# Gate logits out of the attention's own products, all splits on GpSimd, and the first expert choice split in two parts

## The reference, cut to what matters

```python
x = x + tanh(g_xattn[0]) * xattn0(layernorm(x), ctx)       # one head, softmax over 120 keys
x = x + tanh(g_ffn[0]) * moe(layernorm(x))
x = x + tanh(g_xattn[1]) * xattn1(layernorm(x), ctx)       # 16 heads
x = x + tanh(g_ffn[1]) * fp8_linear(layernorm(x))

def moe(x):
    logits = x @ gate_w.T + expert_bias                    # 12 experts
    top, idx = top_k(logits, 2); w = softmax(top)
    # experts 0..7: y = silu(x @ w1.T) @ w2.T, experts 8..11: y = x
    return sum of w * y over the two chosen
```

## Time and profile before

| | |
|---|---|
| median of three executions | 374.39 us |
| the profiled execution, first to last instruction | 378.3 us |
| TensorE, VectorE, ScalarE, GpSimd busy | 92%, 69%, 58%, 41% |
| granted TensorE clock, mean | 0.964 |

### The profile page before, as it was taken

How to read it: one execution, slowest core, us unless ns; L and a number is a source line. 1 busy time by engine, 2 the same in 40 slices (tenths; PEclk the granted TensorE clock), 3 DMA queues, 4 the chain that set the end, 5 groups by cost and what they waited for, 6 DMA issues and landing times.

```text
span 378.3 us, 9027 instructions
## 1 busy us (share of the span) xinstructions
PE 348.3 (92%) x2959; PEld 279.9 (74%) x2960; DVE 261.1 (69%) x659; ACT 219.8 (58%) x452; POOL 154.3 (41%) x197
## 2 busy tenths in 40 slices
PE   3997889988999999999999998879999999998995
PEld 2776769756799999999999994556676667666674
DVE  2588984685646556654554447888789888957696
ACT  2589856742444544554454452456767787774586
POOL 6279967204355556555555535412130331101100
PEclk9999975598999999999999999999999999999999
DMA  6999902221133333322322213410110100000005
GB/s 180 327 413 419 419 30 83 86 84 49 50 99 111 125 108 102 123 83 71 81 69 76 76 40 114 154 57 2 57 58 11 50 2 2 2 5 0 2 28 196
DMA packets 15386, 38.25 MB, mean 101 GB/s; under 512 B 3574, under 2 KB 4748, under 8 KB 13820
## 3 DMA queue, kind: packets, MB, share of 16 engines
q1 hardware_dynamic: 10556, 26.74, 19.5%
q0 software_dynamic: 3936, 10.45, 9.4%
q10 hardware_dynamic: 864, 0.66, 0.6%
HBM read 24.34 MB, written 13.50 MB: 100 GB/s over the span
## 4 chain that ended last, share of the span: by engine, by line
PE 77%; DVE 12%; ACT 5%; DMA 3%; issue 2%; POOL 0%; POOLq 0%
PE two L1964 15%; PE two L1977 14%; PE two L2113 5%; PE two L1996 4%; PE two L2143 4%; PE two L2178 4%; PE two L2099 4%; PE two L2079 3%; PE two L1814 2%; PE two L1987 2%; PE two L2170 2%; PE two L1790 1%; DVE negmax L1133 1%; DMA ident<-in_c_ident 1%; PE two L2159 1%
## 5 line engine op out<-in xcount | busy, mean ns | idle before, releaser
L1364 DVE SCALAR_TENSOR_TENSOR gate<-th,two 128x512 f32<-128x512 f32 x39 | 26.8, 688 | 58.3 <-ACT th L842 32.5
L842 ACT ACTIVATE th<-two 128x512 f32<-128x512 f32 x39 | 23.4, 599 | 71.0 <-PE two L1977 52.8
L585 POOL DMA_INDIRECT y_d<-y_sb,goal_i x39 | 38.5, 988 | 50.4 <-ACT y_sb L852 50.4
L579 POOL DMA_INDIRECT xg<-xn_d,slot_i x39 | 38.0, 974 | 32.3 <-DVE slot_i L1315 14.8
L1964 PE MATMUL two<-wh,gh 128*128 x156 | 44.2, 283 | 0.1
L1964 PE MATMUL two<-wh,gl 128*128 x156 | 44.0, 282 | 0.0
L1964 PE MATMUL two<-wl,gh 128*128 x156 | 43.8, 281 | 0.0
L599 POOL TENSOR_TENSOR rstd<-var,half 128x2 f32<-128x2 f32 x14 | 9.9, 708 | 76.7 <-DVE var L1431 76.7
L1464 DVE TENSOR_REDUCE nm<-two 128x8 f32<-128x960 f32 x32 | 36.1, 1152 | 4.5 <-PE two L2099 4.1
L544 POOL TENSOR_TENSOR wl<-wl,wh 128x512 fp32r<-128x512 f32 x26 | 34.2, 1337 | 8.1 <-ACT wh L726 8.1
L1977 PE MATMUL two<-wh,xh 128*128 x78 | 34.2, 438 | 1.4 <-DVE xl L1358 1.4
(11 more groups left out here) (298 smaller groups left out, 883.3 us busy)
## 6 DMA issues: line engine op xcount, KB each, us to landing
wl<-in_wmoe SPq DMA_DIRECT2D x8, 1024.0 KB, 14.2
y_d<-wh SPq DMA_DIRECT2D x4, 1024.0 KB
yg<-y_d SPq DMA_DIRECT2D x7, 512.0 KB, 3.4
xn_d<-xq SPq DMA_DIRECT2D x8, 256.0 KB, 2.0
xz<-xn_d SPq DMA_DIRECT2D x8, 256.0 KB
out_x<-of SPq DMA_DIRECT2D x8, 256.0 KB, 2.0
x_sb<-in_x SPq DMA_DIRECT2D x1, 1024.0 KB, 10.1
x_sb<-in_x SPq DMA_DIRECT2D x1, 768.0 KB, 4.7
```

Of the source, the lines that this page charges most:

```text
L579: pool.indirect_dma_start(xg[:, n % 2, :], None, xn_d, bass.IndirectOffsetOnAxis(ap=slot_i[:, n:n + 1], axis=0)).then_inc(gathered[n % 2], 16)
L585: pool.indirect_dma_start(y_d, bass.IndirectOffsetOnAxis(ap=goal_i[:, n:n + 1], axis=0), y_sb[:, n % 2, :], None).then_inc(y_stored[n % 2] ...
L842: nc.scalar.activation(th[:], bank[2 + k][:], ACT.Tanh, scale=0.5).then_inc(th_ok, 1)
L1364: dve.scalar_tensor_tensor(gate[:, k, :], th[:], 1.0, bank[2 + k][:], ALU.add, ALU.mult).then_inc(gate_ok, 1)
```

## The change

- The keys of each batch get 12 more columns, which hold the centred gate weights (kq, pitch KP), and the values 12 more, which hold the values times the gate (vg, VP). So scores0 and attend give the gate's product with old x and with the attention's result; VectorE keeps the first (xgate), adds the second in add_x1, and logits_of multiplies the sum by the inverse root. The bias is added later, for seven batches at once and for the last by itself. transpose_x1, copy_xT1 and gate_of go.
- The bias and gain of the values go into their matmul (a second, two-row matmul), and ScalarE copies the values instead of VectorE.
- Each row of x has its inverse root and its negative mean times that root beside it (pitch XP = 258). Rows are stored unnormalised; norm_of normalises each gathered block on VectorE. norm1 goes. The reloads of xz go too: the loop scales x in place (keep_x, add_x).
- All 32 low parts are GpSimd's, in another order. Its inverse roots come one batch at a time, each behind two or one splits; ten splits stand behind the last root and ahead of the first gather, four more between the first gathers.
- VectorE makes the first choice for 14 tiles between the logits of batch 6 and those of batch 7, and for the last two tiles behind them. The maxima are scaled by two 1-wide products instead of one 2-wide with two tensors.
- TensorE waits for 25 low parts ahead of the expert loop's start, and for all 32 ahead of its first pair of second-layer products.

The diff, cut to its core:

```diff
+XP = D + 2
+KP = LK + 12
+VP = D + 12
...
-        ROOTS0, ROOTS1 = ((0, 1), (1, 4), (4, 8)), ((0, 2), (2, 4), (4, 6), (6, 7), (7, 8))
+        ROOTS0, ROOTS1 = ((0, 1), (1, 4), (4, 6), (6, 8)), tuple((b, b + 1) for b in range(B))
...
-        VECTOR_LOW = (6, 10, 14, 18, 22, 26)
+        FIRST_LAYER = [j for j in range(20, CHUNKS) if j % 4 < 2]
+        SECOND_LAYER = [j for j in range(20, CHUNKS) if j % 4 > 1]
+        HIGHS = list(range(20)) + FIRST_LAYER + SECOND_LAYER
+        LOWS = list(range(19)) + FIRST_LAYER + [19] + SECOND_LAYER
...
+            def low(n):
+
+                pool.wait_ge(split_h, HIGHS.index(LOWS[n]) + 1)
+                c = cols(LOWS[n], CHUNK)
                 pool.tensor_tensor(wl[:, c], wl[:, c].bitcast(F32), wh[:, c], ALU.subtract).then_inc(split_l, 1)
+
+            def lows(lo, hi):
+                for n in range(lo, hi):
+                    low(n)
...
+            root1(3)
+            lows(12, 14)
+            root1(4)
+            lows(14, 16)
+            root1(5)
+            low(16)
+            root1(6)
             low(17)
-            for j in range(19, 22):
-                low(j)
-            for j in range(23, 25):
-                low(j)
-            root1(1)
-            low(25)
-            low(27)
-            root1(2)
-            for j in range(28, 30):
-                low(j)
-            root1(3)
-            low(30)
-            root1(4)
-            low(31)
+            root1(7)
+            lows(18, 28)
...
+            gather(0)
+            gather(1)
+            lows(28, 30)
+            gather(2)
+            gather(3)
+            low(30)
+            gather(4)
+            low(31)
+            gather(5)
...
+            copy_probT(2)
+            spread_std(5)
+            high(8)
+            copy_v0(3)
+            copy_xT(5)
             high(9)
-            copy_probT(1)
-            for j in range(10, 12):
-                high(j)
-            exp0_of(2)
-            for j in range(12, 14):
-                high(j)
-            copy_probT(2)
-            high(14)
-            exp0_of(3)
+            exp0_of(4)
+            copy_probT(3)
...
+                dve.wait_ge(gsum_done, 1)
+                at = kq[:, :, 0:C * KP].rearrange("p b (c k) -> p b c k", k=KP)[:, :, :, LK:KP]
+                total = bank[4][:, 0:E_ALL].unsqueeze(1).to_broadcast([P, B, E_ALL])
+                for c in range(C):
+                    own_gate = gate_sb[:, c, 0:E_ALL].unsqueeze(1).to_broadcast([P, B, E_ALL])
+                    ins = dve.scalar_tensor_tensor(at[:, :, c, :], total, 2.0 / D, own_gate, ALU.mult, ALU.add)
+                ins.then_inc(gate_ok0, 1)
...
+                at = bank[6 + b % 2][:, 0:U * KP].rearrange("p (u k) -> p u k", u=U)
+                own.mark(dve.tensor_reduce(lowest[:, b % 2, :], at[:, :, 0:LK], AX, ALU.max, negate=True))
+                dve.tensor_copy(xgate[:, b], at[:, :, LK:KP])
                 own.settle()
-                dve.tensor_tensor(negmax[:, b % 2, :], lowest[:, b % 2, :], rstd0[:, b, :], ALU.mult).then_inc(max_done, 1)
+                for u in range(U):
+                    ins = dve.tensor_scalar(negmax[:, b % 2, u:u + 1], lowest[:, b % 2, u:u + 1], rstd0[:, b, u:u + 1], None,
+                                            ALU.mult)
+                ins.then_inc(max_done, 1)
...
+                own.mark(dve.reciprocal(rsum[:], at[:, :, VP]))
                 own.settle()
+                for u in range(U):
+                    dve.scalar_tensor_tensor(xgate[:, b, u, :], at[:, u, D:VP], rsum[:, u:u + 1], xgate[:, b, u, :], ALU.mult,
+                                             ALU.add)
...
+                    ins = dve.tensor_scalar(logit[:, cols(2 * b + u, E_ALL)], xgate[:, b, u, :], x_rstd(2 * b + u), None, ALU.mult)
                 ins.then_inc(logit_kept, 1)
+
+            def bias_logits(lo, hi):
+
+                dve.wait_ge(gate_in, 32)
+                dve.wait_ge(logit_kept, hi)
+                at = logit[:, lo * U * E_ALL:hi * U * E_ALL].rearrange("p (t e) -> p t e", e=E_ALL)
+                dve.tensor_tensor(at, at, gbias_sb[:, 0:E_ALL].unsqueeze(1).to_broadcast([P, U * (hi - lo), E_ALL]),
+                                  ALU.add).then_inc(biased, 1)
...
+            def choose_first(t):
+                highest(0, lg, t)
+                mark_highest(0, lg, t)
+                keep_first(0, t)
+                leave(t)
...
+            logits_of(5)
             add_x1(7)
-            logits_of(5)
             stats1(7)
-            low(22)
             logits_of(6)
-            low(26)
+            bias_logits(0, B - 1)
+            dve.wait_ge(biased, 1)
+            EARLY, LATE, ALL = slice(0, U * (B - 1)), slice(U * (B - 1), TILES), slice(0, TILES)
+            choose_first(EARLY)
             logits_of(7)
-
+            bias_logits(B - 1, B)
             dve.memset(pairs[:, TILES, :], 0.0)
-            dve.wait_ge(logit_kept, B)
-            highest(0, lg)
-            mark_highest(0, lg)
-            keep_first(0)
-            leave()
-            highest(1, left[:])
-            mark_highest(1, left[:])
-            keep_first(1)
+            dve.wait_ge(biased, 2)
+            choose_first(LATE)
+            highest(1, left[:], ALL)
+            mark_highest(1, left[:], ALL)
+            keep_first(1, ALL)
...
+            def norm_of(i, k):
+                wait(dve, gathered[k], 16 * (i + 1))
+                wait(dve, xgT_done, 2 * i + k - 1)
+                dve.tensor_scalar(xq[:, k, :], xg[:, k, 0:D], xg[:, k, D:D + 1], xg[:, k, D + 1:D + 2], ALU.mult,
+                                  ALU.add).then_inc(xq_ok, 1)
...
+                    t = 2 * i + (k - 4)
+                    dve.tensor_scalar(x_tile(t), x_tile(t), keep_x[:, cols(t, 1)], add_x[:, cols(t, 1)], ALU.mult, ALU.add)
...
+                dst = values_bank(b)[0:LK, 0:VP]
+                pe.matmul(dst, ctxT_sb[:, cols(b, LK)], vg[:], start=True, stop=False, skip_group_check=True)
+                pe.matmul(dst, pair1[:, 0:LK], bv2[:], start=False, stop=True, skip_group_check=True).then_inc(v0_done, 1)
...
+                    dst = bank[6 + b % 2][:, u * KP:(u + 1) * KP]
                     for c in range(C):
-                        ins = pe.matmul(dst, xT[:, b, c, u, :], kq[:, b, cols(c, LK)], start=False, stop=c == C - 1,
-                                        skip_group_check=True)
+                        pe.matmul(dst, xT[:, b, c, u, :], kq[:, b, cols(c, KP)], start=c == 0, stop=False,
+                                  skip_group_check=True)
+                    ins = pe.matmul(dst[:, 0:LK], spread0[:, b % 2, u, :], kq[:, b, C * KP:C * KP + LK], start=False,
+                                    stop=True, skip_group_check=True)
...
+            transpose_x0(4)
+            transpose_prob(2)
+            values0(3)
+            attend(2)
+            scores0(4)
+            transpose_x0(5)
+            transpose_prob(3)
+            values0(4)
+            attend(3)
+            scores0(5)
...
-            pe.wait_ge(split_l, CHUNKS - len(VECTOR_LOW))
-            pe.wait_ge(split_d, len(VECTOR_LOW))
+            pe.wait_ge(split_l, LOWS.index(FIRST_LAYER[-1]) + 1)
...
+            pe.wait_ge(split_l, CHUNKS)
```

613 lines of the change are left out of this document (278 added, 335 removed).

## The result

The changed kernel took 389.65 us (median of 4 executions, 388.36 to 392.78) against 374.41 for the kernel before on the same chip (4 executions, 371.9 to 377.45): a ratio of 1.043, 95% interval 1.034 to 1.052. It is slower. The forecast of 380.5 had the direction, the range of 369 to 386.5 did not hold the time. All ratios leave out executions that took over 1.5% more than the fastest of their kernel; the medians do not.

What follows compares the result with a forecast made beforehand. The prediction took the front ahead of the expert loop as deciding, TensorE having no idle time in the loop. Pairs 4.6 us later, clock 1.0 and ramp 0.5 made 384.4 of span 378.3, less 3.9 gave 380.5 us; range 369 to 386.5.

Steps and rivals of the forecast that it cites:

- the mechanism: Choice of experts: ten GpSimd splits take turns with VectorE's two-SBUF-input operations, so pairs stand at 82.6, 4.6 us later.
- the 12-wide products: Products making the logits on VectorE, one SBUF input: taken as not held by splits, 0.37 us for two.
- The alternative with two more turns: If the 12-wide logits products are held as well, the second choice runs after the last split; pairs at 83.6.
- the last batch: End of the attention: last batch's statistics, then logits(6) done at 67.1, where before the logits waited until 73.4.
- My chain of 5.5 us a batch: Attention, from one attend to the next: scores, transposes, copies, high part, exponentials, attend and handovers take 5.5 us.
- third rival: Attention: the clock falls early, adding 3.5 us from 52 on or 9 from 38 on; 384 to 390, chance 0.13.
- Behind the pairs: From pairs to the end: 1.0 us for TensorE's half clock plus 0.5 for splits and normalised rows among the gathers.
- the clock's 1.0: From pairs to slots: TensorE at half clock after a 12 us wait, 1.0 us taken between 0 and 4.
- The ramp: First gathers and transposes: two splits between gathers and normalised rows cost +0.5 us, bounds -0.5 and +2.5.
- the same difference on it: Span to median: the kernel before's median lay 3.9 us below its span; the same taken off 384.4 gives 380.5.
- the first (no hold): Choice of experts: splits do not hold it, pairs at 73.7, 4.3 us ahead; 370.1 us, between 367 and 373, chance 0.25.
- The second (a quicker attention): Attention: a cycle of 4.7 us, last batch 3 to 5 us earlier; 376.5, between 373 and 378.5, chance 0.17.

Runs made afterwards that it cites:

- Experiment 5: Changed kernel with all splits, but biased logits, eq, cand and left in PSUM instead of SBUF; median 385.02 us, ratio 1.033.
- experiment 8: Changed kernel with 52 more 128x512 TensorE filler matmuls in the wait for the pairs; median 388.62 us.
- experiment 1: Kernel before, unaltered, profiled a second time; full clock all through, span 8.3 us shorter than in the first trace, pairs 8.35 us earlier.
- experiments 2: Changed kernel with the ten splits ahead of the first gather subtracting only 2 of 512 columns; median 379.80 us, ratio 1.023.
- experiment 6: Changed kernel with ScalarE's copy of transposed probabilities moved ahead of exponentials and high parts, batches 3 to 7; median 383.86 us, ratio 1.027.
- the kernel with filler: Kernel before with eight 128x512 TensorE filler matmuls in three waits of the attention; median 372.67 us against 372.31, ratio 1.002.

## Why the prediction was wrong

**Right: the mechanism and where it strikes.** Ten splits behind the last root, each trading a turn with one operation of the choice: ten held operations were forecast and ten came, though not the same ten, since the first equality and the two 12-wide products took turns that I had given to the operations at the end. The splits end at 81.1 (forecast 81.4), pairs at 83.65 (82.6). That early choice is worth nothing, that reductions stay short, that the clock is at half when the pairs come: all as forecast. The splits themselves were not lengthened to 1.4, they stayed at 1.26; that they end where forecast is that error against a start 0.6 us later than forecast (68.5 instead of 67.9).

**One term wrong by 1.0 us: the 12-wide products.** I took them as not held, after the logits of before, which read PSUM. They were held, 2.33 us for two. The alternative with two more turns had 83.6 for the pairs, and 83.65 was measured; that it agrees so closely is in part luck, by the offsetting errors just named. Experiment 5 shows the other side: with one input in PSUM nothing is held. By the Trainium skill (VectorE: DVE Perf Modes, "Mode 2×_2P") a product of one fp32 tensor in SBUF reads it through both ports, and these traces agree that it contends like an operation with two SBUF inputs.

**Right by two errors: the last batch.** Its logits(6) end at 67.7, forecast 67.1. My chain of 5.5 us a batch was too long; at full clock it is 5.11, and the logits(6) then end at 66.0 (experiment 5). And the clock fell in the attention of the profiled execution (0.87 from 30 to 40 and 0.79 from 40 to 50), which gave 1.7 us back. That was the third rival's place, at a fifth of its price: its 384 to 390 holds the measured time, but not for its reason.

**Wrong: "Behind the pairs".** I had added 1.0 for the clock and 0.5 for the ramp to the 300.3 us from pairs to the end. Measured were 304.8, so 4.4 us more. Only 0.3 of them lie between pairs and slots (9.05 against 8.75), where I had put the clock's 1.0; the 1.0 of experiment 8 includes what the clock costs behind the slots. The ramp was mis-sized: taken +0.5 between bounds of -0.5 and +2.5, it is about 4.1 from the slots on (1.65 to the first h, 1.4 more to the first y, 1.1 behind), above its own upper bound. Narrowing the four splits among the gathers brings the way from pairs to the end to 301.4, scaling the rows on ScalarE to 301.6. Both undo the same thing: two 256-wide products of one SBUF tensor, held for 2.12 us between gather and transpose, and the idle TensorE behind them at half clock until 105. It is the price of the 12-wide products again, in a place where I had not applied it at all.

**Wrong: the baseline.** These two make 4.0 us: the span came out at 388.4, the sum had 384.4. The other 5.2 us are the step "the same difference on it", from span to median: this span lies 1.3 us below its median, the span of before 3.9 above. This is the largest of the errors, and with it goes the sentence "Before, the transposes and gate products of TensorE kept the logits until 73.4. That is where removing 64 gate matmuls and their transposes pays: some 6 us." That held in the one execution that was profiled, whose clock was at half from 52 on. At full clock, as in the second trace (0.998, and the fastest 30 of 67 executions have 0.991 to 0.999 where it is known), the kernel before has its last logits at 64.9 and its pairs at 69.7, and what these logits waited for last is another engine than in the earlier trace rows (VectorE's timeline of experiment 1):

```profile
64.49 0.37 DVE L1169 SCALAR_TENSOR_TENSOR logit<-two,rstd,gbias_sb 128x12 f32<-128x12 f32 x2 [0.16 <-POOL less L538]
```

It was GpSimd's root, not TensorE's gate products, which had ended 0.7 us before the root. VectorE is busy at 0.94 there and TensorE at 0.74 (60 to 70): the removed matmuls were hidden. So the change had a slow front to win against only in some executions; its own lie at 388.4 to 392.8. Its profiled execution (390.25 us) was near its median of 389.65, while that of before, at about 380.2, stood 5.8 us above its own. A difference between span and median belongs to the execution that was profiled, not to the kernel, and can't be carried over.

**The sum, redone** against the kernel before at full clock (span 370.0), for the 18.4 us: ten splits beside the choice 9.0; the attention of the profiled execution at half clock 1.8; the attention's order and the choice, seen with fourteen splits narrow (72.26 against 69.66), 2.6; behind the pairs 4.4. That is 17.8; 0.6 are not assigned. The terms come from different executions, each with its own clock, so each may be off by some tenths.

The rivals: the first (no hold) is refuted by experiments 2 and 5. The second (a quicker attention) was true by 0.4 us a batch and not by 0.8; experiment 6 reached its pace only by moving the copies.

## What to carry to other kernels

- Count the work that one engine holds against another as a sum that must be placed somewhere: speeding up the choice moved the same splits' turns onto the operations behind it. Twelve splits or eight ahead of the gathers made 4.3 us at the slots (with some filler changed too).
- Where an engine beside GpSimd is late, first look where its operands lie. Intermediates in PSUM took 6.4 us off the choice without removing an instruction; 1.6 of them came back on the way to the slots, and the median fell by 4.6.
- Before a difference is computed from one trace, look at the granted clock in it. If the clock fell in a stage that the change removes, the gain exists only in executions like that one; the spread of the times (here 371.9 to 374.4 for three runs beside a span of 378.3) is the warning.

## What the runs showed of the hardware

- VectorE operations with both inputs in SBUF, or fp32 products of one SBUF tensor, wait for one whole GpSimd split each: 0.92 to 1.4 us instead of 0.18 to 0.36, whatever their width (12 to 192 columns). 16-bit comparisons are held as well (1.76 instead of 0.81). The 1-wide products are not: the changed kernel's sixteen of the row maxima took 0.20 to 0.21 us each, two of them at 58.91, within the splits of 57.13 to 59.62, where the 2-wide product of two tensors before took up to 1.13. That part of the change does work, though no run prices it alone.
- GpSimd loses little to short operations: ten splits took 12.62 us held against and 12.34 where most of the choice read PSUM, but 13.09 beside held operations of 192 columns, and one took 1.73 instead of 1.27 behind a subtraction of 128x512.
- The Trainium skill (SBUF — State Buffer, "SBUF: two separate sides") has the lock for two SBUF inputs against a GpSimd operation that reads SBUF; these traces agree, and show that against splits in a row it goes turn by turn.
- One kernel, one core: executions fell in three groups of times, 9 us from the fastest to the slowest. The slowest group goes with the granted clock (0.964 in all of it), with nearly the same work up to the fall. The middle one does not go with it alone: it has means from 0.975 to 0.993, and 0.993 to 0.998 in the kernel with filler.
